# Ternary comparisons inside the chunks of layer 0, and six steps of a four-layer kernel put in another order

## The reference

```python
def ternary_quant(w_fp32, g=64):
    w_g = w.reshape(-1, g)
    scale = jnp.clip(jnp.mean(jnp.abs(w_g), axis=-1, keepdims=True), 1e-08, None)
    q = jnp.clip(jnp.round(w_g / scale), -1, 1)
    return w + (q * scale - w)
```

## Time and profile before

| | |
|---|---|
| median of three runs | 656.05 us |
| profiled execution | 656.43 us, of which the span is 654.5 us |
| TensorE busy | 629.6 us (96% of the span) |
| VectorE, ScalarE, GpSimd busy | 516.1, 335.1, 336.3 us |
| chain that ended last | TensorE 68%, ScalarE 11%, VectorE 9%, issue 8%, GpSimd 2% |
| mean granted TensorE clock | 0.992 |

### The profile page before, as it was taken

How to read it: one execution, slowest core, us unless ns; L and a number is a source line. 1 busy time by engine, 2 the same in 40 slices (tenths; PEclk the granted TensorE clock), 3 DMA queues, 4 the chain that set the end, 5 groups by cost and what they waited for, 6 DMA issues and landing times.

```text
span 654.5 us, 13468 instructions
## 1 busy us (share of the span) xinstructions
PE 629.6 (96%) x4850; PEld 502.6 (77%) x4850; DVE 516.1 (79%) x1093; ACT 335.1 (51%) x747; POOL 336.3 (51%) x267
## 2 busy tenths in 40 slices
PE   8999999999989999999999999998997899999997
PEld 3446788788668989888898888887986765868786
DVE  4478776693889999999999989676663689969995
ACT  1597212202466565765656555465634466159851
POOL 2063555584378487584848736998456325230000
PEclk9999999999999999999999999999999699999999
DMA  8902000012301011010100001111313100100001
GB/s 245 380 2 76 1 2 1 3 41 97 113 18 41 26 27 38 8 40 16 40 24 22 26 18 52 49 30 41 140 47 99 35 23 1 42 0 2 0 1 66
DMA packets 14954, 31.56 MB, mean 48 GB/s; under 512 B 1885, under 2 KB 8763, under 8 KB 14333
## 3 DMA queue, kind: packets, MB, share of 16 engines
q1 hardware_dynamic: 13229, 27.41, 12.8%
q0 software_dynamic: 1536, 3.15, 1.7%
q10 hardware_dynamic: 144, 0.40, 0.2%
HBM read 26.76 MB, written 5.24 MB: 49 GB/s over the span
## 4 chain that ended last, share of the span: by engine, by line
PE 68%; ACT 11%; DVE 9%; issue 8%; POOL 2%; another core or an unknown queue 1%; ACTq 0%; DVEq 0%; POOLq 0%
PE bank L658 9%; PE bank L660 8%; PE bank L659 8%; PE bank L648 7%; PE bank L639 5%; PE bank L1224 4%; PE bank L893 3%; PE bank L923 3%; PE bank L924 3%; ACT arena L1506 2%; DVE arena L1987 2%; ACT arena L1486 2%; PE bank L908 2%; PE bank L1267 2%; DVE x L2007 2%
## 5 line engine op out<-in xcount | busy, mean ns | idle before, releaser
L658 PE MATMUL bank<-zone 128*128 128x256 f32 (+1 forms) x472 | 165.7, 351 | 5.5 <-POOL zone L2485 3.0
L660 PE MATMUL bank<-zone 128*128 128x256 f32 (+1 forms) x472 | 157.1, 333 | 0.0
L659 PE MATMUL bank<-zone 128*128 128x256 f32 (+1 forms) x472 | 157.0, 333 | 0.0
L2526 POOL TENSOR_TENSOR arena<-arena 128x512 f32<-128x512 f32 x64 | 82.3, 1286 | 60.2 <-ACT arena L1486 53.1
L658 PEld LDWEIGHTS bank<-zone 128*128 128x128 f32 x472 | 89.9, 190 | 21.5 <-issue 10.1
L660 PEld LDWEIGHTS bank<-zone 128*128 128x128 f32 x472 | 89.8, 190 | 9.0
L659 PEld LDWEIGHTS bank<-zone 128*128 128x128 f32 x472 | 90.2, 191 | 6.1
L2531 POOL TENSOR_TENSOR arena<-arena 128x512 f32<-128x512 f32 x64 | 83.9, 1312 | 15.6 <-DVE arena L1978 7.7
L1506 ACT ACTIVATE arena<-arena 128x256 f32<-128x256 f32 (+1 forms) x128 | 62.0, 488 | 21.5 <-DVE arena L1987 18.6
L1977 DVE TENSOR_TENSOR arena<-bank,arena 64x512 f32<-64x512 f32 x64 | 44.4, 693 | 22.0 <-ACT arena L1486 20.3
L2007 DVE SCALAR_TENSOR_TENSOR x<-bank,arena,x 128x256 f32<-128x256 f32 x128 | 53.2, 473 | 8.1 <-PE bank L660 7.5
(11 more groups left out here) (307 smaller groups left out, 1277.8 us busy)
## 6 DMA issues: line engine op xcount, KB each, us to landing
arena<-in_qk SPq DMA_DIRECT2D x16, 256.0 KB, 2.7
arena<-in_tern SPq DMA_DIRECT2D x1, 3072.0 KB, 21.9
arena<-in_wv SPq DMA_DIRECT2D x8, 256.0 KB, 2.9
arena<-in_wo SPq DMA_DIRECT2D x16, 128.0 KB, 2.1
arena<-in_wr SPq DMA_DIRECT2D x1, 1792.0 KB, 7.2
lB<-in_lB SPq DMA_DIRECT2D x1, 1288.5 KB, 24.6
xg_rows<-arena SPq DMA_DIRECT2D x1, 1024.0 KB
arena<-in_cossin SPq DMA_DIRECT2D x2, 512.0 KB, 4.7
```

Source lines behind the costliest of these rows:

```text
L658: pe.matmul(dst, lhi, rhi, start=(n == 0), stop=False)
L659: pe.matmul(dst, lhi, rlo, start=False, stop=False)
L660: last = pe.matmul(dst, llo, rhi, start=False, stop=(n == len(terms) - 1 and not open_end))
L2526: pool.tensor_tensor(qraw[:, j, :], qraw[:, j, :], cosT[:, at], ALU.mult).then_inc(cos_done, 1)
```

## The change

- `ternary_signs(n)` moves into chunk n + 1, between the running sum (L1917) and `hidden0(n + 1, 1)`, for n = 0 to 5; none is left after the chunks. GpSimd's `by_parity` copies are placed to suit, and the inverse deviation moves out of part 5, behind `rest_of_wv(0)`.
- The table load moves ahead of `keep_raw(0, 2)`. `rest_of_wqk(1)` moves ahead of the second half of `turn_qk(0)`.
- `rest_of_wo(h)` moves ahead of the second lot of row sends.
- The first group of `hidden_of(2)` moves ahead of `gates3(1)`, whose two banks are now the first two of the other four.
- `project_h` does both tiles with `hre` first, and waits for `him` behind them. The last pair is split in two groups in two banks, one for each tile.

```diff
-        g_gate3.append(groups(gate3_ready, 2)[::-1])
+        g_gate3.append([group(gate3_ready, SUMS[n]) for n in range(2)][::-1])
+        g_last3 = group(x_added, SUMS[1])
...
             hidden_of(1)
             project_in(1)
+            hidden_of(2, [0])
             gates3(1)
...
-                for tt in range(2):
-                    for k, part in enumerate((hre, him)):
+                for k, (part, ready) in enumerate(((hre, hre3_ready), (him, h3_ready))):
+                    pe.wait_ge(ready, 1)
+                    for tt in range(2):
...
-                hidden_of(n)
+                hidden_of(n, [1] if n == 2 else range(2))
...
-            pe.wait_ge(hre3_ready, 1)
-            pe.wait_ge(h3_ready, 1)
             project_h(0)
...
-            for p in range(1, NT // 2):
+            for p in range(1, NT // 2 - 1):
                 project_h(p)
+            for tt in range(2):
+                project_last_h(tt)
...
             keep_affinities(1)
+            load_exponential()
             keep_raw(0, 2)
             keep_raw(0, 3)
             round_wqk(1)
-            keep_v(0, some=range(2, 3), bank=2)
-            load_exponential()
-            keep_v(0, some=last_one, bank=2)
+            keep_v(0, some=range(2, NT // 2), bank=2)
...
                     dve.tensor_tensor(kvbd[:, c + 1, :], kvbd[:, c, :], kvtmp, ALU.add).then_inc(kvbd_ready, 1)
+                    if c:
+                        ternary_signs(c - 1)
                 hidden0(c, 1)
...
-                if c % 2 == 0:
-                    ternary_signs(c // 2)
-            ternary_signs(4)
             dve.wait_ge(*g_sum0.ready)
             dve.reciprocal(oinv0, oinv0).then_inc(oinv_ready, 1)
-            ternary_signs(5)
...
+            by_parity(2)
             for n in range(6):
-                for c in (2 * n + 1, 2 * n + 2):
-                    if 2 <= c < NT:
-                        by_parity(c)
+                if n + 3 < NT:
+                    by_parity(n + 3)
...
-                if n == 5:
-                    inverse_deviation(1, 0)
-                    pool.wait_ge(xn_ready, NT + TPB)
...
-            inverse_deviation(1, 1)
+            inverse_deviations(1)
             pool.wait_ge(cs_loaded, 32)
             pool.wait_ge(xn_ready, 2 * NT)
             turn_qk(0, range(2))
             pool.wait_ge(score_ready, NB)
+            rest_of_wqk(1)
             turn_qk(0, range(2, 4))
-            rest_of_wqk(1)
...
                 turn_qk(h + 1, (0, 1), base)
+                rest_of_wo(h)
                 between()
-                rest_of_wo(h)
                 turn_qk(h + 1, (2, 3), base)
```

More of the change, by code:

```diff
@@ L1214, in _, with hidden_of @@
             project_z2(3)
-            def hidden_of(n):
+            def hidden_of(n, some=range(2)):
                 b, q = divmod(n, NI)
-                for i, g in enumerate(g_gu3[n]):
+                for i in some:
+                    g = g_gu3[n][i]
                     reuse(g)
@@ L1307, in project_h, with project_last_h @@
                 reuse(g)
-                for tt in range(2):
-                    for k, part in enumerate((hre, him)):
+                for k, (part, ready) in enumerate(((hre, hre3_ready), (him, h3_ready))):
+                    pe.wait_ge(ready, 1)
+                    for tt in range(2):
                         last = pe.matmul(g.ps[:, tt * D:(tt + 1) * D], part[:, tok(2 * p + tt)], lD[:, D_OUT + k * D:D_OUT + (k + 1) * D],
-                                         start=(k == 0), stop=(k == 1))
+                                         start=(k == 0 and tt == 0), stop=(k == 1 and tt == 1), skip_group_check=True)
+                last.then_inc(g.full_sem, 1)
+            def project_last_h(tt):
+                g, t = (g_out3[-1], g_last3)[tt], NT - 2 + tt
+                reuse(g)
+                for k, part in enumerate((hre, him)):
+                    last = pe.matmul(g.ps[:, 0:D], part[:, tok(t)], lD[:, D_OUT + k * D:D_OUT + (k + 1) * D], start=(k == 0), stop=(k == 1))
                 last.then_inc(g.full_sem, 1)
             for n in range(2, UNITS):
-                hidden_of(n)
+                hidden_of(n, [1] if n == 2 else range(2))
                 if n < AHEAD:
@@ L1534, in keep_affinities, with load_exponential @@
                 act.activation(affT[:, b * BW:(b + 1) * BW], g_affT[b].ps[0:ER, :], ACT.Sigmoid, bias=lB[0:ER, B_BIAS:B_BIAS + 1]).then_inc(g_affT[b].ready_sem, 1)
+            def load_exponential():
+                act.activation(small[:, 14:15], small[:, 10:11], ACT.Exp)
             round_wqk(0)
@@ L1549, in _ @@
             round_wqk(1)
-            keep_v(0, some=range(2, 3), bank=2)
-            def load_exponential():
-                act.activation(small[:, 14:15], small[:, 10:11], ACT.Exp)
             most, last_one = range(NT // 2 - 1), range(NT // 2 - 1, NT // 2)
-            load_exponential()
-            keep_v(0, some=last_one, bank=2)
+            keep_v(0, some=range(2, NT // 2), bank=2)
             head(0, 0)
@@ L2447, in _ @@
             add_out3(2)
[L2448 to L2451, removed]
+            x_is(g_out3[-1].ready[1] - 1)
+            for tt, g in enumerate((g_out3[-1], g_last3)):
                 t = NT - 2 + tt
-                dve.tensor_tensor(x[:, t, :], x[:, t, :], g.ps[:, tt * D:(tt + 1) * D], ALU.add).then_inc(g.ready_sem, 1)
+                dve.wait_ge(*g.full)
+                dve.tensor_tensor(x[:, t, :], x[:, t, :], g.ps[:, 0:D], ALU.add).then_inc(g.ready_sem, 1)
         @block.gpsimd
```

## The result

The changed kernel took 659.69 us (median of 6 runs, 657.92 to 660.29), the kernel before on the same chip 655.96 us (6 runs). The ratio is 1.0045, 95% interval 1.0027 to 1.0062: slower by more than the 0.2% that can be told from nothing. The forecast was 657.8 us, ratio 1.0027. The profiled execution took 659.59 us, 657.7 of them span; before it was 656.43 and 654.5 us.

A forecast was written before the change was run, and what follows sets the result against it. TensorE, busy for 96% of the span, was taken to bound the kernel. A's +6.3 less 2.65, 1.05, 0.05, 0.44 and 0.37 for B to F gave +1.74 on 656.05: 657.8 us, range 650.2 to 660.3.

The forecast's parts named there:

- The likeliest case: Layer 0 chunks: VectorE and GpSimd take turns, masks come late, later gains don't pay for it; 657.8 us, chance 0.64.
- no meeting: Rival, layer 0 chunks: the engines' meeting doesn't hurt TensorE, no mask is late; -5.6 us, 650.4 us, chance 0.25.
- a lower clock in the chunks: Rival: TensorE's idle lowers its clock to 1.2 GHz in chunks 5 to 7, each some 8 us longer; 680, chance 0.02.
- the gains behind are eaten: Rival: late rotation in the first head and GpSimd in heads 12 to 14 eat gains; 2.1 us left, 660.3, chance 0.09.
- B: Start of head 0: table load and head 1's weight rest go earlier, TensorE's two waits shrink or go; gain 2.65 us.
- C: Head 11: the rest of the output weights starts ahead of two row sends, TensorE's wait goes; gain 1.05 us.
- A: Layer 0 chunks: ternary comparisons moved into chunks 1 to 6 meet GpSimd's passes, making masks late; costs 6.3 us net.
- The chain of turns: Layer 0 chunks: VectorE and GpSimd alternate whole instructions, giving a cycle of 11.0 us against TensorE's 8.97.
- T: Layer 0 chunks: the end of a part's comparisons, forecast at 84.0, 94.5, 105.5, 116.5 and 127.5 us from chunk 2 on.
- D: Layer 3: four matmuls fill the idle ahead of the gates, but TensorE then waits longer for VectorE; gain 0.05 us.
- E: Last outputs: matmuls on the real part go ahead of the wait for the imaginary part; gain 0.44 us.
- F: Very end: the last pair's first tile fills sooner, so its addition is done before the second is full; gain 0.37 us.

The follow-up runs named there:

- Short passes: The changed kernel with GpSimd's four passes over each part cut to one of its 16 groups; 651.6 us, one run, first chip.
- part A alone: The kernel before with only the two orders in the chunks and the inverse deviation's place changed; 663.03 us (1.011) first chip, 649.09 us (1.0077) third.
- part B alone: The kernel before with only the table load and head 1's weight rest moved earlier in head 0; 641.29 us, ratio 0.9958, second chip.
- without part A: The changed kernel with VectorE's and GpSimd's earlier orders in the chunks put back; 653.53 us, ratio 0.9963, first chip.
- only part 0 moved: The changed kernel with only part 0's comparisons moved, into chunk 1, the other parts as before; 651.96 us (0.9938) first chip, 637.93 us (0.9897) third.

## Why the prediction was right, point by point

The likeliest case came true: the two engines meet in every chunk, TensorE waits for masks from chunk 4 on, and what is won behind doesn't pay for it. Both rivals of no meeting and of a lower clock in the chunks fell: from chunk 3 on comparisons took 3.16 us each, and the clock there was full. The Trainium skill, SBUF — State Buffer, section Who interferes with whom, has a VectorE instruction with two SBUF inputs and a GpSimd instruction that reads SBUF contend for a lock that one of them holds alone; the trace agrees (3.16 us and 3.01 in strict turns). Short passes took the waits away altogether. The rival that the gains behind are eaten, 660.3 us, lies nearer to the measured 659.69 than my 657.8 does, and still isn't what happened: it had one thing right, the late second half of the rotation, which took 0.85 us, but B and C kept most of their gains. The sum came out well on the chips where it could be seen by itself, +1.5 against +1.74. That it did so within 0.2 us is partly luck: A was 0.8 to 1.0 us too dear and B 0.65 to 0.85 too good, and the two errors cancel. On the first chip 659.69 is inside the range, 0.6 us from its end, for a reason that had no term.

- **A, 6.3 for 5.3 to 5.5.** The chain of turns was right, for the parity copies too. Two sizes were off. The cycle is 10.8 us for 11.0: T is 94.38 there, and the second pass ends at 98.71, 4.3 us behind it where I had 4.6; the sum of 98.33 waits for that end, and all that follows in the chain is some 0.3 us sooner. And the step "chunk 7 ... needs its mask 0.6 us sooner: ... 2.6 late" named the wrong instruction: TensorE waits there for the bank of VectorE's second hidden product of chunk 6 (1.45 us, L1881), and then 0.40 for a mask. From start to start chunks 4 to 7 are 0.77, 1.82, 1.81 and 2.15 us longer than their 8.97 and 8.52: 6.55 us for my 7.1 to 7.2, and less chunk 1's 1.1 about 5.4. (The idle times shown, 5.45 us in all, are smaller, as they are counted from the modelled ends of the matmuls.)
- **B, 2.65 for 1.8 to 2.0.** "So nothing waits, and the whole shifts by 2.65 us" was true for the first 4 us (2.86) and then failed: the copies of the expert scores and the rotation now come in one heap on VectorE, and head 1 gets 0.85 back. I had looked at what the moved instructions delay on GpSimd, not at what the readers of the earlier scores find on VectorE. The table load also came in front of the copy, and its cover held: the wait it left is 0.30 us.
- **C, 1.05.** 1.0 to 1.2 in head 11 on all chips. Then 0.40 is given back on the first chip. On the other two, the kernels with C gain some 0.4 more in head 13, where part A alone and part B alone show a wait of 0.35 us for GpSimd that they haven't.
- **D, 0.05, E 0.44 and F 0.37** were right: D's 0.87 us went at a wait for VectorE (0.59), which was nearly always busy, E gave 0.45 and F 0.37.
- **The 1.9 us above the forecast** are mostly clock. In the profile, the step from +2.58 to +4.26 is 0.36 us of a longer wait and 1.33 of TensorE at 1.2 GHz behind it; against the wait stand 0.35 us less in the stretch near 510. I had put 0.02 on a lower clock, in the chunks, and had no term for it elsewhere. Five of the six runs had this lower mean clock, and the sixth was 1.8 us above the kernel before at the same clock, near the forecast's 1.74. On the other chips, where the clock was full, the changed kernel ran at +1.5 us. So of the 3.7 us that make it slower on the first chip about half are the order's own and half are clock; on the others the change makes no difference by the median, because the kernel before loses clock there in 23 of 38 runs and the changed one in none of 11.
- **Open:** what ScalarE and VectorE wait for at head 13 on the first chip ("remote"). In all six profiles there ScalarE goes on 0.94 to 1.02 us after the last of GpSimd's four early row sends, and with part C, where these end later beside TensorE's scores, TensorE's wait is longer (2.04 to 2.09 us for 1.69 and 1.72). But on the other chips ScalarE goes on while the sends still run (448.02 in the changed kernel, the last one until 450.29), so the sends alone don't hold it; the experiment that moves them ran where the wait doesn't occur. Open too is why the clock fell behind it in the changed kernel's profile. The wait's length isn't the reason by itself: in the profiles without part A, with short passes and with only part 0 moved TensorE waited 2.08, 2.09 and 2.04 us and the clock stayed full. The stretch behind the wait without part A (columns as in the earlier trace rows):

```profile
446.00:450.00 4.00, 3.38 (x22) 2.93 (x23) 0.99 (x5) 4.00 (x14) 3.84 (x4) 1.00 0.02 4
```

## What to carry to other kernels

Before moving SBUF-to-SBUF work of VectorE under a phase that looks covered, lay it beside GpSimd's long instructions of the same phase and play the turns out: here 2.4 us of comparisons became 6.3, and moving only the part whose comparisons stood in the way, instead of all six, gained 1.2 to 1.6 us where all six lost 5.3 to 5.5. When a wait is removed, follow the work that the freed engine now feeds sooner, on the engine that reads it. And a few tenths of a per cent should be compared at the same granted clock and on more than one chip.

## What the runs showed of the hardware

- The same kernel can wait on one chip where it doesn't on another. The changed kernel's span is 657.7 us on the first and 642.7 on the third with the same instructions. 3.9 us of it are at head 13, waiting and lower clock together, and 10.8 between 501.9 and 522.3: TensorE waits for issue there seven times, 4.9 us, and its weight loads 7.7, with the clock at 0.50 from 511 to 520; on the other chip TensorE's waits in the same work (497.7 to 507.4) are 0.2 us and the clock is full. Two rows of the first chip by stretch, columns as in the earlier trace rows:

```profile
508.00:511.00 3.00, 0.91 (x5) 0.38 (x5) 0.69 (x1) 0.96 (x4) 2.39 (x3) 0.95 0.51 105
511.00:514.00 3.00, 1.89 (x8) 0.55 (x7) 1.25 (x3) 0.00 (x0) 2.28 (x3) 0.50 0.36 100
```

  and one of the other:

```profile
508.00:511.00 3.00, 2.92 (x30) 2.73 (x29) 1.83 (x6) 1.47 (x4) 2.52 (x4) 1.00 0.42 105
```

  The DMA moves 105 GB/s in both rows of 508 to 511. TensorE, VectorE and ScalarE thin out together on the first chip, as if their instructions came late; that is argued, not shown.
- A GpSimd copy of f32 from SBUF to SBUF takes turns with VectorE too: 0.40 us alone, 1.27 beside a comparison.
- The mean granted clock of a run takes few values: 0.995, 0.992, 0.989 and 0.986 on the first chip (each to within 0.001), some 1.4 us of time apart, 1.000 and 0.997 on the others, 1.7 apart.
